# A gated cross-attention and mixture-of-experts layer on one core: two late routings taken apart into single steps, their exponentials computed on GpSimd, and one more gather for each shared unit

## The reference, cut to what matters

```python
x = x + tanh(g_xattn) * attention(layernorm(x), ctx)
xn = layernorm(x)
weights = softmax(xn @ gW + gb)              # 15 experts
topv, topi = top_k(weights, 3)
routed = sum_k topv[k] * expert[topi[k]](xn)
x = x + tanh(g_ffn) * (shared_expert(xn) + routed + xn)
```

## Time and profile before

| | us |
|---|---|
| median of 3 runs | 503.03 |
| the runs | 500.92 to 503.83 |
| the profiled execution | 499.99 |
| its span, first to last instruction | 498.2 |

### The profile page before, as it was taken

How to read it: one execution, slowest core, us unless ns; L and a number is a source line. 1 busy time by engine, 2 the same in 40 slices (tenths; PEclk the granted TensorE clock), 3 DMA queues, 4 the chain that set the end, 5 groups by cost and what they waited for, 6 DMA issues and landing times.

```text
span 498.2 us, 11929 instructions
## 1 busy us (share of the span) xinstructions
PE 391.1 (79%) x3870; PEld 349.5 (70%) x3870; DVE 306.4 (62%) x1015; ACT 277.0 (56%) x612; POOL 231.0 (46%) x238
## 2 busy tenths in 40 slices
PE   4586989897989898877887999898999999991000
PEld 2374868676868687767887988788989899991000
DVE  2634567868687777855565778576666546643231
ACT  4355778787778868765464555555555564430000
POOL 6601131267476557534233453044445345557772
PEclk9758899999999999997989999999999999996555
DMA  7589566273535354524567998888989513222221
GB/s 175 163 231 243 138 158 125 105 198 117 150 124 154 109 145 139 158 91 132 137 173 223 284 320 252 222 259 239 270 262 270 167 31 82 59 62 73 74 73 47
DMA packets 69014, 80.11 MB, mean 161 GB/s; under 512 B 10265, under 2 KB 60185, under 8 KB 68953
## 3 DMA queue, kind: packets, MB, share of 16 engines
q1 hardware_dynamic: 60120, 63.08, 45.3%
q0 software_dynamic: 6672, 14.30, 9.7%
q10 hardware_dynamic: 2160, 1.97, 1.2%
HBM read 48.02 MB, written 29.29 MB: 155 GB/s over the span
## 4 chain that ended last, share of the span: by engine, by line
PE 48%; DMA 10%; ACT 10%; DVE 8%; issue 8%; POOL 7%; SPq 5%; DVEq 1%; ACTq 1%; POOLq 0%
PE psum L1364 8%; PE psum L1249 5%; PE psum L1232 5%; PE psum L1475 5%; POOL k_heads L585 4%; PE psum L1354 3%; DMA k_split<-k_parts 2%; DMA xnT<-in_packs 2%; PE psum L1355 2%; PE psum L1356 2%; PE psum L1344 2%; PE psum L1267 2%; POOL q_stack L585 2%; ACT q_stack L647 2%; ACT probs L655 2%
## 5 line engine op out<-in xcount | busy, mean ns | idle before, releaser
L528 POOL DMA_INDIRECT rows_by_expert<-xn_all,row_of x96 | 94.1, 980 | 83.7 <-ACT q_parts L725 45.3
L655 ACT ACTIVATE probs<-psum 77x512 f32<-77x512 f32 x128 | 68.8, 587 | 20.4 <-PE psum L1232 19.0
L585 POOL DMA_INDIRECT k_heads<-outs_by_block,back_row x60 | 56.9, 948 | 45.7 <-PE psum L1475 17.1
L1232 PE MATMUL psum<-q_stack,k_heads 128*77 128x128 f32 x512 | 50.4, 244 | 17.1 <-ACT q_stack L647 17.0
L1232 PEld LDWEIGHTS psum<-q_stack,k_heads 128*77 128x77 f32 x512 | 46.0, 158 | 24.0 <-ACT q_stack L647 23.3
L830 DVE TENSOR_REDUCE max_cols<-psum 128x4 fp32r<-128x312 f32 x128 | 55.3, 474 | 10.6 <-PE psum L1209 10.5
L1354 PE MATMUL psum<-q_parts,w_ring 128*128 128x256 f32 x152 | 50.0, 329 | 13.9 <-ACT probs L733 11.9
L961 DVE CAST w_ring<-w 128x512 fp32r x76 | 38.9, 512 | 29.9 <-issue 21.5
L725 ACT ACTIVATE q_parts<-psum 128x256 fp32r<-128x256 f32 x76 | 29.1, 384 | 34.2 <-PE psum L1344 26.3
L952 DVE TENSOR_TENSOR q_parts<-psum,q_parts 128x256 fp32r<-128x256 f32 x76 | 32.0, 422 | 26.1 <-ACT q_parts L725 25.0
L1354 PEld LDWEIGHTS psum<-q_parts,w_ring 128*128 128x128 f32 x152 | 29.5, 194 | 19.8 <-issue 15.4
(11 more groups left out here) (168 smaller groups left out, 950.3 us busy)
## 6 DMA issues: line engine op xcount, KB each, us to landing
w_raw<-rows_by_expert SPq DMA_DIRECT2D x76, 128.0 KB
outs_by_block<-probs SPq DMA_DIRECT2D x76, 128.0 KB, 3.6
q_stack<-q_split SPq DMA_DIRECT2D x21, 256.0 KB
q_split<-q_parts SPq DMA_DIRECT2D x8, 512.0 KB
k_heads<-k_split SPq DMA_DIRECT2D x96, 39.0 KB
xn<-in_packs SPq DMA_DIRECT2D x19, 193.0 KB
xnT<-in_packs SPq DMA_DIRECT2D x19, 193.0 KB, 3.7
k_parts<-in_packs SPq DMA_DIRECT2D x19, 193.0 KB
```

Of the source, the lines that this page charges most:

```text
L528: nc.gpsimd.indirect_dma_start(xd[:, :], bass.IndirectOffsetOnAxis(ap=row_of[:, r, m:m + 1], axis=0), xn2_all[:, r * GB + m // K, :], None ...
L585: nc.gpsimd.indirect_dma_start(back[j][:, m, :], None, yd[half][:, :], bass.IndirectOffsetOnAxis(ap=back_row[:, j, b * K + k:b * K + k + 1 ...
L655: nc.scalar.activation(probs[0:KV, n % 2, hg * 512:(hg + 1) * 512], st_ps[hg % 2][0:KV, :], ACT.Exp, scale=SCALE).then_inc(exp_done, 1)
L1232: ins = nc.tensor.matmul(st_ps[hg % 2][0:KV, hh * S:(hh + 1) * S], k_heads[:, g % 2, hg, hh, b, 0:KV], q_stack[:, g % 2, hg, b * S:(b + 1) ...
```

## The change

- The exponentials of the router for the last two groups leave ACT. POOL computes them as e to the power of `shifted`, in two halves of two sequences each (`pow_logits`, 128 partitions x 36 elements), after the scatters that are paired with blocks 0 and 1 (group NG - 2) and 12 and 13 (group NG - 1). A GELU of two values (`gelu_probe`) stands on ACT ahead of the blocks.
- `choose` is split into `largest` and `indices`, `place` into `mark` and `weigh`; the steps of the last two routings are spread over blocks 0 to 20, where they took blocks 0 to 10. The second half's table moves from blocks 11 to 15 to blocks 22, 24, 26 and 28, with PE and DVE in the same iteration; `back_rows` from 17 to 24 to 29 to 36; `add_base` from 25 to 32 to 14 to 18, 21, 23 and 25.
- The 15 pads of the second half were issued by ACT in blocks 15 to 29. Eight are now issued by ACT in blocks 24 to 31, seven by SP in blocks 27 to 33.
- In the shared expert POOL does five gathers for each unit. Group 4 is combined after unit 6, groups 5 and 6 after unit 7.
- The last group's gathers run by sequence, its three k inside; each sequence is combined and stored by itself.

```diff
--- before.py
+++ after.py
@@ -94,6 +94,8 @@
         ident_sb = sb("ident_sb", [P, P])
         ident_r = sb("ident_r", [P, P], F32R)
         half_pow = sb("half_pow", [P, GB])
+        euler = sb("euler", [P, 1])
+        gelu_probe = sb("gelu_probe", [P, 2])
...
-        last_in = [sem(f"last{k}_in") for k in range(K)]
+        last_in = [sem(f"last{b}_in") for b in range(GB)]
...
+                if 27 <= u < 27 + E - 8:
+                    sp.wait_ge(pads_ready, 2)
+                    pad_rows(1, 8 + u - 27)
...
-            for j in range(NG):
+            for j in range(NG - 1):
                 sp.wait_ge(combined, (j + 1) * K)
                 sp.dma_start(out[j * GB:(j + 1) * GB, :, :].rearrange("b t d -> t b d"), x_all[:, j * GB:(j + 1) * GB, :]).then_inc(out_done, 16)
-            sp.wait_ge(out_done, NG * 16)
+            for b in range(GB):
+                sp.wait_ge(combined, (NG - 1) * K + (b + 1) * K)
+                sp.dma_start(out[B - GB + b, :, :], x_all[:, B - GB + b, :]).then_inc(out_done, 16)
+            sp.wait_ge(out_done, (NG - 1 + GB) * 16)
...
-                k, b = divmod(m, GB)
-                nc.gpsimd.indirect_dma_start(back[j][:, m, :], None, yd[half][:, :],
-                                             bass.IndirectOffsetOnAxis(ap=back_row[:, j, b * K + k:b * K + k + 1], axis=0)).then_inc(back_in[j] if j < NG - 1 else last_in[k], 16)
+                if j < NG - 1:
+                    k, b = divmod(m, GB)
+                else:
+                    b, k = divmod(m, K)
+                nc.gpsimd.indirect_dma_start(back[j][:, k * GB + b, :], None, yd[half][:, :],
+                                             bass.IndirectOffsetOnAxis(ap=back_row[:, j, b * K + k:b * K + k + 1], axis=0)).then_inc(back_in[j] if j < NG - 1 else last_in[b], 16)
+
+            def pow_logits(r, first, end):
+                pool.wait_ge(route_step, r * ROUTE + 4)
+                ins = nc.gpsimd.tensor_tensor(expd[:, first:end], euler[:].unsqueeze(2).broadcast_to([P, end - first, E + K]), shifted[:, first:end], ALU.pow)
+                if end == GB:
+                    ins.then_inc(soft_exp, 1)
 
             later = [(NG - 3, m) for m in range(1, GB * K)] + [(r, m) for r in (NG - 2, NG - 1) for m in range(GB * K)]
             for u, (r, m) in enumerate(later):
                 pool.wait_ge(xs_hi_ready, u + 1)
                 scatter(r, m, m + 1)
                 if u == 0:
+                    pow_logits(NG - 2, 0, GB // 2)
+                if u == 1:
                     pow2(NG - 1)
+                    pow_logits(NG - 2, GB // 2, GB)
+                if u == 12:
+                    pow_logits(NG - 1, 0, GB // 2)
+                if u == 13:
+                    pow_logits(NG - 1, GB // 2, GB)
             in_blocks = NU - NB - 4
             for n in range(in_blocks):
                 pool.wait_ge(xs_hi_ready, NB + 4 + n + 1)
                 gather(n)
             for n in range(in_blocks, NG * GB * K):
-                j, part = divmod(n - in_blocks, 4)
+                j, part = divmod(n - in_blocks, 5)
                 if j < NG:
-                    pool.wait_ge((s_l1, s_l1, s_gelu, s_l2)[part], (j * CS + 1, j * CS + 3, j * CS + 4, j + 1)[part])
+                    pool.wait_ge((s_l1, s_l1, s_gelu, s_gelu, s_l2)[part], (j * CS + 1, j * CS + 3, j * CS + 2, j * CS + 4, j + 1)[part])
...
-            exp_logits(NG - 2)
+            act.wait_ge(tanh_done, 1)
+            nc.scalar.activation(gelu_probe[:], tanh_g[:], ACT.Gelu)
             for u in range(NU):
                 gelu(u)
-                if u == 2:
-                    apply2(NG - 1, 0, GB)
-                if u == 4:
+                if 4 <= u < 6:
+                    apply2(NG - 1, (u - 4) * 2, (u - 3) * 2)
+                if u == 7:
                     lead_x2(NG - 1)
-                if u == 7:
-                    exp_logits(NG - 1)
-                if u == 15:
+                if u == 24:
                     act.wait_ge(pads_ready, 2)
-                if 15 <= u < 15 + E:
-                    pad_rows(1, u - 15)
+                if 24 <= u < 32:
+                    pad_rows(1, u - 24)
...
             def choose(r):
-                done = r * ROUTE
-                dve.wait_ge(route_step, done + 1)
+                largest(r)
+                indices(r)
+
+            def largest(r):
+                dve.wait_ge(route_step, r * ROUTE + 1)
                 for b in range(GB):
                     ins = nc.vector.max(top[:, b, :], logits[:, b, :])
                 ins.then_inc(route_step, 1)
+
+            def indices(r):
+                done = r * ROUTE
...
             def place(r):
+                mark(r)
+                weigh(r)
+
+            def mark(r):
...
+            def weigh(r):
+                done = r * ROUTE
+                dve.wait_ge(route_step, done + 6)
                 dve.wait_ge(soft_exp, r + 1)
...
+            def combine_last(b):
+                j, t = NG - 1, B - GB + b
+                dve.wait_ge(last_in[b], K * 16)
+                dve.wait_ge(s_added, NG)
+                for k in range(K):
+                    if k >= 1:
+                        dve.wait_ge(combined, j * K + b * K + k)
+                    nc.vector.scalar_tensor_tensor(x_all[:, t, :], back[j][:, k * GB + b, :], gate_of[:, t, k:k + 1], x_all[:, t, :],
+                                                   ALU.mult, ALU.add).then_inc(combined, 1)
+
             def combine(j, k):
-                if j < NG - 1:
-                    dve.wait_ge(back_in[j], GB * K * 16)
-                else:
-                    dve.wait_ge(last_in[k], GB * 16)
+                dve.wait_ge(back_in[j], GB * K * 16)
...
                 if u == 0:
                     residual(B - 1)
                     stats2_of(B - 1)
+                if u == 1:
                     var2_of(NG - 1)
-                if u == 1:
+                if u == 2:
+                    mark(NG - 2)
+                if u == 3:
                     shift2_of(NG - 1)
-                if u == 2:
-                    place(NG - 2)
-                if u == 3:
+                if u == 7:
+                    trail_x2(NG - 1)
+                if u == 8:
+                    weigh(NG - 2)
+                if u == 9:
                     add_base_row(NG - 2)
+                if u == 10:
                     rows(NG - 2)
-                if u == 4:
-                    trail_x2(NG - 1)
-                if u == 6:
+                if u == 11:
                     add_bias(NG - 1)
-                    choose(NG - 1)
-                if u == 8:
-                    place(NG - 1)
-                if u == 10:
+                    largest(NG - 1)
+                if u == 12:
+                    indices(NG - 1)
+                if u == 13:
+                    mark(NG - 1)
+                if u in (14, 15, 16, 17, 18, 21, 23, 25):
+                    add_base((14, 15, 16, 17, 18, 21, 23, 25).index(u))
+                if u == 19:
+                    weigh(NG - 1)
+                if u == 20:
                     add_base_row(NG - 1)
                     rows(NG - 1)
-                if 12 <= u < 16:
-                    table(1, u - 12)
-                if 17 <= u < 17 + 8:
-                    back_rows(u - 17)
-                if 25 <= u < 25 + NG:
-                    add_base(u - 25)
+                if u in (22, 24, 26, 28):
+                    table(1, (u - 22) // 2)
+                if 29 <= u < 29 + 8:
+                    back_rows(u - 29)
                 if NB + 1 <= u < NB + 9:
                     back_rows(u - NB + 7)
...
-                for i in ((0,), (1,), (), (2,), (3,), (), (), (4, 5, 6, 7))[j]:
+                for i in ((0,), (1,), (), (2,), (3,), (), (4,), (5, 6))[j]:
                     for k in range(K):
                         combine(i, k)
+            for b in range(GB):
+                combine_last(b)
...
-                if u == 2:
+                if u == 6:
+                    pe.wait_ge(route_step, (NG - 2) * ROUTE + 1)
+                    turn_x2(NG - 1)
+                if u == 9:
+                    pe.wait_ge(x2_lo_ready, NG)
                     ranks(NG - 2)
-                if u == 4:
+                if u == 10:
                     pe.wait_ge(route_step, (NG - 2) * ROUTE + 12)
-                    turn_x2(NG - 1)
-                if u == 5:
                     token_logits(NG - 1)
-                if u == 9:
+                if u == 20:
                     ranks(NG - 1)
-                if 11 <= u < 15:
-                    table(1, u - 11)
+                if u in (22, 24, 26, 28):
+                    table(1, (u - 22) // 2)
```

More of the change, by code:

```diff
@@ L503, in _ @@
             pool.memset(half_pow[:], -0.5)
+            pool.memset(euler[:], math.e)
             pool.memset(zeros[:], 0.0).then_inc(zeroed, 1)
```

## The result

The changed kernel takes **479.55 us** (median of 4 runs, 478.30 to 481.14) where the kernel before, run beside it, takes 503.29 (4 runs, 500.92 to 503.83): ratio 0.953, interval 0.950 to 0.956. The forecast was 481.4 with a range of 474 to 496. The profiled execution took 481.14 us (span 479.3), against 499.99 (498.2) of before. It lies 1.6 above its median where the one of before lay 3.3 under its own, so the two traces differ by 18.9 us of span and the medians by 23.7.

The account below looks back on a forecast made before the run. Prediction: the first blocks (PE waiting for GELUs, place and table steps) and the tail (POOL's dense gathers) were the places to gain. Terms -2.6, -15.5, +3.2, +2, -8.7, 0 sum to -21.6: 478.4 profiled, 481.4 us median, range 474 to 496.

Parts of the forecast that it names:

- Start, -2.6: Start of the blocks: the small GELU loads its tables earlier, removing PE's wait of 2.6 us.
- Blocks 1 to 15, -15.5: Early blocks: GELU, place and table waits go, so 15 steps take 31.5 us instead of 47.05.
- Powers, +3.2: POOL's exponentials: 7.1 us for each half, bounded by 1.05 and 9.4; waits of 0.5 and 2.7 us in blocks.
- Rival D: Each power on POOL stops DVE, and PE drops to its lower clock: 509.6 us, slower than before; chance 0.12.
- Rival A: The power on POOL is cheap, near 1.05 us, with no wait anywhere: 478.2 us; chance 0.12.
- Rival B: The power on POOL is dear, 9.4 us, with waits of 12.4 in place of 3.2: 490.6 us; chance 0.12.
- Rival C: Early blocks fall only to 2.5 us each, held by packs or DVE: 487.4 us; chance 0.10.
- Rival E: Shared expert: the fifth gather does not fit and the tail stays: 490.1 us; chance 0.04.
- Pads and moved steps in blocks 16 to 37, +2: SP's pads cost about 0.55 us each, up to 1.4 in all; back rows in blocks 32 to 36 about 0.6.
- the wait of 2.7: Block 19: DVE's `weigh` waits 2.7 us for POOL's last power half, part of the powers' +3.2.
- Gathers, -8.7: Tail: five gathers a unit leave 28 instead of 35 in the dense row, at 1.25 us each, saving 8.7 us.
- Last group, 0: Tail: three dependent combinations replace four independent ones behind the last gather, with a smaller last store; no change in time.

Follow-up runs that it names:

- Experiment 5: Changed kernel with both exponentials back on ACT, no small GELU and no powers on POOL, steps still spread: 484.79 us, ratio 0.965.
- Experiment 6: Changed kernel with every half of the power computed twice, first into a spare buffer: 505.94 us, ratio 1.008 to the kernel before.
- experiment 7: Changed kernel with one undivided power of 72 elements for each group in place of two halves: 488.09 us, ratio 0.971.
- experiment 4: Changed kernel with four gathers for each shared-expert unit again instead of five: 490.67 us, ratio 0.981.
- Experiment 1: Changed kernel with all 15 second-half pads issued by ACT, two for each of blocks 24 to 31, none by SP: 479.83 us, ratio 0.958.
- experiment 2: Experiment 1's kernel with SP also reading the seven pad row numbers without using them: 479.72 us, ratio 0.957.
- experiment 3: Experiment 1's kernel with SP also issuing seven 128 KB writes of zeros to fixed rows: 480.47 us, ratio 0.963.
- experiment 12: Changed kernel with pads spread thin, ACT one in each of blocks 24 to 35, SP three, on a third chip: 483.23 us, ratio 0.960.
- experiment 8: Changed kernel reading each pad's row number one iteration earlier, on a chip where the kernel before takes 513.68 us: 518.43 us, ratio 1.009.

## Why the prediction was right, and where it was off

- *Start, -2.6:* the mechanism held (table load at 219.13, ahead of the first GELU). Size -1.4 in this pair of traces, as the attention ended 1 us later.
- *Blocks 1 to 15, -15.5:* right. 30.45 us for the forecast 31.5, no wait of PE over 0.7, and the clock stayed at its upper level, as I had left inside the term. Experiment 5 shows that the exponentials need not leave ACT for most of it (14.3 of the 16.6); spreading the steps is what counts.
- *Powers, +3.2:* the row was 6.2 for my 7.1, and only 0.5 us was waited for in blocks 16 to 20, which together took 1.1 us more than before and 1.0 more than in experiment 5 without the powers. So this term was about 2 us too large. The bounds of 1.05 and 9.4 held it well. Experiments 6 and 7 show how near the edge is: doubled, they eat the whole gain.
- *Rival D, the power holds DVE:* fell. Experiment 6 puts eight powers into the blocks and only the steps that need them wait. SBUF — State Buffer, "Who interferes with whom", in the Trainium skill says that a DVE copy or cast in its two-port mode and GpSimd block each other; thirteen casts at 0.43 us beside powers of 6.2 do not agree with it, while the subtraction of the earlier trace rows does. No row names the mode of a cast.
- *Rivals A and B:* the power lay between them. *Rival C:* fell with 2.03 us a block. *Rival E:* fell; the fifth gather fits, and POOL still stands 0.43 to 0.87 us in front of each unit's last gather, where 0.30 lies between two dense ones.
- *Pads and moved steps in blocks 16 to 37, +2:* **this is the term that was mis-sized.** The region cost 7.8 (5.8 to 7.3 in the traces of experiments 4, 5 and 7) where +2 and the wait of 2.7 made 4.7, and nearly all of it lies in blocks 28 to 34 (+8.1), those with SP's pads. The step that failed is "a third of a round, about 0.55, so SP's round is 2.2": a pad costs SP 1.13 in the trace, mostly a read of its row number that I did not see because the earlier trace rows has no pad in it, and the round was 3.28. I also took the doubling (ten pads in five blocks, by two issuers) as free. Experiment 1 shows both halves: without its pads SP is ahead again and blocks 28 to 34 lose 4 us or more, but ACT then pays 1.8 for two pads and the gain is gone. Experiments 2 and 3 show that it is not the traffic, 12 that thinner spacing takes 2.1 to 3.6 us off blocks 28 to 31 and that the last pad then comes too late. How much is the read, how much the bunching, stays open: experiment 8 only moved the read to another place on SP's queue, and the blocks kept their pace.
- *Gathers, -8.7:* right, 8.5 in the pair of traces and 8.8 by experiment 4. *Last group, 0:* right, 9.1 us from the last gather's start in either order.

That the median came so near is luck in part. The trace came out 2.7 us above its forecast (-18.9 for -21.6), mostly because blocks 16 to 37 cost 3.1 more than forecast. The median came out 1.9 under its own, because I had added 3.0 for the distance between one execution and the median, and for the changed kernel that distance was -1.6: a second miss of 4.6 us, of the other sign.

## What to carry to other kernels

Cost a step on an issuing queue by the gap from the issue before it to its own, register reads included, and by whether that queue was waiting before: an engine seen waiting for a free buffer has slack, and seven additions of 1.1 us turned this one from ahead to behind. Reading a register value earlier on the same queue only moves its cost. Late work spread over many iterations, with the consumer two blocks behind its producer, is worth more than moving it to another engine (14.3 us with the exponentials still on ACT, against about 5 for moving them). When transfers are spread out, look at who waits for the last of them.

## What the hardware showed that was not expected

- A power on POOL costs 1.05 us for 4 elements a partition, 6.2 for 36 and 11.9 for 72: 0.16 us an element and 0.4 to 0.5 us beside it.
- A power of 6.2 us leaves DVE's casts at 0.43 us, while those beside an indirect transfer of POOL took 0.52 on average and up to 0.67.
- The same instructions ran 2% longer on one chip for the kernel before (513.7 against 502.3 us) and some 8% longer for close kin of the changed kernel (517 to 520 against 480), with waits that the trace gives to no instruction. Why is open, and a gain measured on one chip is a gain there.
- A read of a row number into a register holds SP's queue wherever it stands: in front of the pad (gap 0.78 us) or, an iteration ahead, in front of the pack (gap 0.9 to 1.3, 0.23 without it).
